# First attention of a four-stage kernel: reciprocals repeated by transfers through DRAM and multiplied by GpSimd, keys stored in three transfers

## What is computed

```
x = x + tanh(g_xattn[0]) * L0_xattn(layernorm(x), ctx, Wq, bq, ..., Wo, bo)
x = x + tanh(g_ffn[0])   * L0_ffn(layernorm(x), ...)
x = x + tanh(g_xattn[1]) * L1_xattn(layernorm(x), ctx, ctx, gamma)
x = x + tanh(g_ffn[1])   * L1_ffn(layernorm(x), ...)
```

```
q, k, v = Wq @ x + bq, Wk @ c + bk, Wv @ c + bv      # each (16 heads, 8, 256)
p   = softmax(q^T k / sqrt(8))                       # (16, 256, 256)
out = Wo @ (v p^T) + bo
```

## Time and profile before

| what | us |
|---|---|
| three runs | 737.46, 737.70, 739.45 (median 737.7) |
| span of the profiled execution | 735.7 |
| TensorE busy in it | 652.3 (89%) |
| VectorE busy | 520.7 (71%) |
| ScalarE busy | 371.1 (50%) |
| GpSimd busy | 343.9 (47%) |
| first attention | about 0 to 262 |

### The profile page before, as it was taken

How to read it: one execution, slowest core, us unless ns; L and a number is a source line. 1 busy time by engine, 2 the same in 40 slices (tenths; PEclk the granted TensorE clock), 3 DMA queues, 4 the chain that set the end, 5 groups by cost and what they waited for, 6 DMA issues and landing times.

```text
span 735.7 us, 13724 instructions
## 1 busy us (share of the span) xinstructions
PE 652.3 (89%) x4738; PEld 343.7 (47%) x4738; DVE 520.7 (71%) x1245; ACT 371.1 (50%) x616; POOL 343.9 (47%) x402
## 2 busy tenths in 40 slices
PE   3889999999999989989853789899988899999996
PEld 1233333333333345778530344444443367777763
DVE  3888989888889479936346889899864864333336
ACT  2047778788777644345421556566642203444420
POOL 3745646657431110177376887642010036777630
PEclk9999999999999999999985889999999999999998
DMA  6945545565632293054563677785218312222237
GB/s 151 208 109 138 144 119 140 155 172 148 173 91 82 58 308 80 1 158 142 187 181 99 184 208 220 193 213 166 71 39 268 84 40 68 88 88 81 71 116 255
DMA packets 110151, 101.12 MB, mean 137 GB/s; under 512 B 26344, under 2 KB 95629, under 8 KB 109611
## 3 DMA queue, kind: packets, MB, share of 16 engines
q1 hardware_dynamic: 100259, 80.52, 39.0%
q0 software_dynamic: 8352, 18.74, 9.2%
q10 hardware_dynamic: 1472, 0.99, 0.6%
HBM read 58.49 MB, written 24.40 MB: 113 GB/s over the span
## 4 chain that ended last, share of the span: by engine, by line
PE 58%; DVE 17%; issue 7%; POOL 7%; DMA 5%; SPq 3%; ACT 2%; POOLq 0%; ACTq 0%; DVEq 0%
PE O L478 10%; PE S L433 10%; PE ST L1567 6%; DVE mx L597 5%; POOL spare L305 4%; PE ST L441 3%; PE ST L1481 3%; PE M L1584 2%; PE S L1584 2%; PE M L527 2%; PE M L520 2%; SPq L170 2%; DMA QS<-mxT 1%; DMA PX<-xn,TI 1%; PE M L1512 1%
## 5 line engine op out<-in xcount | busy, mean ns | idle before, releaser
L597 DVE TENSOR_REDUCE mx<-S 128x2 f32<-128x512 f32 x384 | 251.2, 684 | 37.9 <-PE S L433 36.4
L353 ACT ACTIVATE PX<-ST 128x1024 f32<-128x1024 f32 x192 | 196.2, 1024 | 95.9 <-PE ST L441 91.6
L433 PE MATMUL S<-QS 62*128 62x256 bf16 (+1 forms) x768 | 151.8, 293 | 37.7 <-DVE mx L597 29.9
L441 PE MATMUL ST<-QS 64*128 64x256 bf16 (+1 forms) x768 | 141.1, 278 | 2.6 <-DMA QS<-mxT 2.6
L478 PE MATMUL O<-PX,VA 128*32 128x256 f32 x1536 | 123.9, 395 | 0.1
L433 PEld LDWEIGHTS S<-QS 62*128 62x128 bf16 (+1 forms) x768 | 48.1, 97 | 156.8 <-DVE mx L597 104.7
L305 POOL DMA_INDIRECT spare<-ye,GI x64 | 67.9, 1060 | 25.0 <-issue 12.7
L1685 POOL DMA_INDIRECT PX<-xn,TI x39 | 39.8, 1020 | 54.4 <-DVE K1n L1874 38.9
L441 PEld LDWEIGHTS ST<-QS 64*128 64x128 bf16 (+1 forms) x768 | 54.0, 97 | 17.5 <-issue 9.0
L810 POOL DMA_INDIRECT PX<-xn,TI x32 | 34.1, 1064 | 53.5 <-DVE spare L1196 44.1
L1567 PE MATMUL ST<-EGU,Cb 128*128 x156 | 52.7, 460 | 0.3 <-ACT Cb L1640 0.3
(11 more groups left out here) (299 smaller groups left out, 1111.4 us busy)
## 6 DMA issues: line engine op xcount, KB each, us to landing
QS<-QKs SPq DMA_DIRECT2D x93, 128.0 KB
QS<-keys SPq DMA_DIRECT2D x16, 512.0 KB, 4.7
keys<-spare SPq DMA_DIRECT2D x96, 64.0 KB, 2.1
QS<-QKs SPq DMA_DIRECT2D x93, 64.0 KB
EGU<-in_ew SPq DMA_DIRECT2D x16, 256.0 KB, 4.5
xn<-spare SPq DMA_DIRECT2D x8, 512.0 KB, 10.3
ye<-QKc SPq DMA_DIRECT2D x32, 128.0 KB, 2.1
VA<-in_val SPq DMA_DIRECT2D x16, 256.0 KB, 2.9
```

The costliest lines, as they stand in the source:

```text
L353: e.activation(M["PX"][pair % 4][:, :], M["ST"][pair % 2][:, :], ACT.Exp, scale=A.scale).then_inc(A.exp, 1)
L433: got = e.matmul(M["S"][n % 2][:, 256 * a:256 * a + 256], QS[:, 0, 128 * a:128 * a + 128], QS[:, 1, :], start=True, stop=True)
L441: got = e.matmul(M["ST"][(NP * t + k // 2) % 2][:, 512 * u + 256 * a:512 * u + 256 * a + 256], QS[:, 1, 128 * a:128 * a + 128], QS[:, 0, : ...
L597: e.tensor_reduce(M["mx"][b % 2][:, :, A.row_of_max(head)], M["S"][n % 2][:, :].rearrange("p (a s) -> p a s", a=2), AX.X, ALU.max, negate= ...
```

## The change

For the batches 0 to 13 of the first attention (`by_rows`) the reciprocals go another way. Batches 14 and 15, and the second attention, keep the old one.

- VectorE takes the reciprocals of batch t-1 behind the maximum of k=6 of step t, not those of batch t-2 behind k=0.
- SP stores them to DRAM (`den_d`, 4 rows of 4 KB) at the end of its list of the same step, ahead of the keys.
- In the next step, between the third and the fourth `spread`, SP repeats the 4 rows 8 times each from DRAM to DRAM (`row_d`, 32 rows of 4 KB), where it stored `rT` before. Behind `dn` and `on` it waits for this to have landed and loads `row_d` into `RB`, 128x256.
- GpSimd multiplies `on` by `RB` at the end of its step. The matmul of line 520 and VectorE's multiplication of line 634 are gone.
- `output` stays at k=15 of the same step. `rT` is now the first 16 rows of `RB`.
- The keys are stored by three transfers in place of six. Each repeats one part over 3, 2 or 1 of the rows k. The array in DRAM has k ahead of the rows i, and the loads and the two stores of constants follow it.
- One semaphore (`gates`) is merged into another (`filled`).

```diff
+    def by_rows(self, b):
+        return self.first and 0 <= b < NB - 2
...
 def keys_stored(e, w, A, M, b):
     w.wait_ge(A.keys, 4 * (b + 1))
-    rows = M["keys_d"][b].rearrange("(i k) (g t) -> i g k t", k=8, g=8)
-    for k in range(6):
-        e.dma_start(rows[:, :, k, :], M["KW"][b % 2][:, TERMS[k][1], :]).then_inc(A.kept[b % 2], 16)
+    rows = M["keys_d"][b].rearrange("k i (g t) -> (i g) k t", g=8)
+    for j, lo, hi in ((0, 0, 3), (1, 3, 5), (2, 5, 6)):
+        part = M["KW"][b % 2][:, j, :].unsqueeze(1).to_broadcast([P, hi - lo, T // 2])
+        e.dma_start(rows[:, lo:hi, :], part).then_inc(A.kept[b % 2], 16)
...
 def attention_sp(...):
         def reciprocals():
             w.wait_ge(A.rr, b5 + 1)
-            w.wait_ge(A.rb, b5 - 1)
+            if A.first:
+                w.wait_ge(A.on, b5 - 1)
+            else:
+                w.wait_ge(A.rb, b5 - 1)
             e.dma_start(M["rT"][b5 % 2][0:H, :], M["rdn"][:, 0:2 * H]).then_inc(A.rT, 16)
+        def repeated():
+            w.wait_ge(A.rT, 16 * (b5 + 1))
+            w.wait_ge(A.rows, 32 * (b5 - 1))
+            e.dma_start(M["row_d"][b5 % 2].rearrange("(j i) x -> j i x", j=4),
+                        M["den_d"][b5 % 2].unsqueeze(1).to_broadcast([4, A.R, NQ * T])).then_inc(A.rows, 16)
...
                 spread(e, A, M, b1, k)
-                if k == 2 and within(b5) and A.first:
-                    reciprocals()
+                if k == 2 and A.by_rows(b5):
+                    repeated()
...
+        elif A.by_rows(b5):
+            repeated()
         elif within(b5) and not A.late(b5):
             reciprocals()
...
             e.dma_start(on[b4 % len(on)][:, :], M["OS"][0:P:NQ, 0:NQ, :]).then_inc(A.num, 16)
+        if A.by_rows(b5):
+            w.wait_ge(A.rows, 32 * b5 + 16)
+            w.wait_ge(A.on, b5 - 1)
+            e.dma_start(M["RB"][b5 % 2][:, :], M["row_d"][b5 % 2].rearrange("r (g t) -> (r g) t", g=NQ)).then_inc(A.rows, 16)
...
+        if A.by_rows(b4):
+            w.wait_ge(A.rr, b4 + 1)
+            e.dma_start(M["den_d"][b4 % 2], M["rdn"][:, 0:2 * H]).then_inc(A.rT, 16)
         if A.first and within(t + 1):
             keys_stored(e, w, A, M, t + 1)
...
 def attention_pool(...):
         if A.first and within(t + 2):
             keys(t + 2)
+        b5 = t - 2
+        if A.by_rows(b5):
+            on = M["on" + A.name][b5 % 2]
+            w.wait_ge(A.rows, 32 * (b5 + 1))
+            w.wait_ge(A.num, 16 * (b5 + 1))
+            e.tensor_tensor(on[:, :], on[:, :], M["RB"][b5 % 2][:, :], ALU.mult).then_inc(A.on, 1)
...
 def attention_pe(...):
-                if k == 12 and within(b5):
+                if k == 12 and within(b5) and not A.by_rows(b5):
                     denominators(b5)
...
 def attention_dve(...):
-                if k == 0 and within(b5):
+                if k == 0 and within(b5) and not A.by_rows(b5):
                     reciprocals(b5)
+                if k == 6 and A.by_rows(t - 1):
+                    reciprocals(t - 1)
...
-                if k == 13 and within(b5):
+                if k == 13 and within(b5) and not A.by_rows(b5):
                     normalized(b5)
```

More of the change, by code:

```diff
@@ L96, in __init__ @@
             self.kp, self.yb = one("kp"), one("yb")
+            self.rows = one("rows")
             self.vt, self.va = one("vt"), one("va")
@@ L265, in keys @@
         w.wait_ge(A.ldc[b % U], 16 * (b // U + 1))
-        w.wait_ge(A.kept[b % 2], 96 * (b // 2))
+        w.wait_ge(A.kept[b % 2], 48 * (b // 2))
         w.wait_ge(A.keys, 4 * b)
@@ L518, in denominators @@
         w.wait_ge(A.rT, 16 * (A.n0 + b + 1))
+        if A.first:
+            w.wait_ge(A.on, b)
         bank()
@@ L632, in normalized @@
         w.wait_ge(A.num, 16 * (A.n0 + b + 1))
-        w.wait_ge(A.rb, b + 1)
+        w.wait_ge(A.rb, b + 1 - (NB - 2 if A.first else 0))
         e.tensor_tensor(on[:, :], M1[:, 256:512], on[:, :], ALU.mult).then_inc(A.on, 1)
@@ L732, in __init__ @@
         self.again = [one(f"again{u}") for u in range(E0 - PLACES)]
-        self.again0 = [96 * NB // 2, 96 * NB // 2, 32, 0, 0]
+        self.again0 = [48 * NB // 2, 48 * NB // 2, 32, 0, 0]
         self.at = {}
@@ L751, in ffn0_sp @@
     for k in (6, 7):
-        e.dma_start(M["keys_d"].rearrange("b (i k) x -> k (b i) x", k=8)[k],
-                    d["hole"][:, 3072:4096].to_broadcast([NB * P // 8, 1024])).then_inc(B.kept[2], 16)
+        e.dma_start(M["keys_d"][:, k, :, :],
+                    d["hole"][:, 3072:4096].unsqueeze(1).to_broadcast([NB, P // 8, 1024])).then_inc(B.kept[2], 16)
     w.wait_ge(G.dve, G.at["wd"])
@@ L760, in stack_ready @@
         for k in range(2):
-            w.wait_ge(B.kept[k], 96 * NB // 2)
+            w.wait_ge(B.kept[k], 48 * NB // 2)
         w.wait_ge(B.kept[2], 32)
@@ L2075, in allocate @@
                           ("st6", [P, 6], F32), ("mv", [P, 2], F32), ("ve", [P, 1], F32), ("rs", [P, 1], F32),
-                          ("mx", [P, 2, 16], F32), ("mxT", [16, T], BF16), ("rT", [16, T], F32), ("on", [P, T], F32)):
+                          ("mx", [P, 2, 16], F32), ("mxT", [16, T], BF16), ("RB", [P, T], F32), ("on", [P, T], F32)):
         M[nm] = [sb(f"{nm}{n}", shape, dt) for n in range(2)]
+    M["rT"] = [m[0:16, :] for m in M["RB"]]
     Cbs = sb("Cb", [P, U, T])
@@ L2160, in allocate @@
     M["ye_d"] = nc.dram_tensor("ye", [E0 * CAP + P, T], F32, kind="Internal").ap()
-    M["keys_d"] = nc.dram_tensor("keys", [NB, P, 4 * T], F32, kind="Internal").ap()
+    M["keys_d"] = nc.dram_tensor("keys", [NB, 8, P // 8, 4 * T], F32, kind="Internal").ap()
+    for nm, rows in (("den", 4), ("row", 32)):
+        two = nc.dram_tensor(nm, [2, rows, 4 * T], F32, kind="Internal").ap()
+        M[nm + "_d"] = [two[n] for n in range(2)]
     M["ew_d"] = d["ew"]
@@ L2212, in build @@
         M["n_e"] = 16 * (EARLY + 3)
-        hole, filled, gates, gamma = (sem(nm) for nm in ("hole", "filled", "gates", "gamma"))
+        hole, filled, gamma = (sem(nm) for nm in ("hole", "filled", "gamma"))
         M["hole"], M["gamma"] = hole, gamma
@@ L2299, in act_program @@
             w.wait_ge(M["w_g"], 16)
-            e.activation(M["tg"][:, :], M["graw"][:, 0:4], ACT.Tanh).then_inc(gates, 1)
+            w.wait_ge(filled, 1)
+            e.activation(M["tg"][:, :], M["graw"][:, 0:4], ACT.Tanh).then_inc(filled, 1)
             attention_act(e, w, L0, M, ffn0_act_meanwhile(e, w, X, L0, M))
@@ L2336, in gated @@
                 if t == -3 and k == 1:
-                    w.wait_ge(gates, 1)
+                    w.wait_ge(filled, 2)
                     e.tensor_tensor(M["tg"][:, 2:3], M["tg"][:, 2:3], M["graw"][:, 4:5], ALU.mult).then_inc(gamma, 1)
```

2 lines of the change are left out of this document (1 added, 1 removed).

## The result

The changed kernel takes 758.07 us in the median of four runs (755.32 to 758.79), beside 738.4 for four of the kernel before: a ratio of 1.0257 with a 95% interval of 1.0226 to 1.0289, or 19.7 us slower. Forecast were 749.9 us and a range up to 756. The direction and the main mechanism were right, the size was not.

What follows compares the result with a forecast made beforehand. TensorE and VectorE take turns setting the pace through two banks S. 13 steps, each 1.14 less 0.11 us longer, give 13.4; less 1.2 at the start, +12.2 us: 749.9 us, range 735 to 756.

Steps and rivals of the forecast that it cites:

- Parts 1 and 2: First attention, line 520's matmul and VectorE's multiplication gone: together 0.05 to 0.11 us a step gained, 0.11 taken.
- Part 3: Reciprocals at k=6 wait for the transfer of `dn`: maximum of k=7 1.14 us late in each of 13 steps.
- Part 4: SP's queue: a shorter list ends TensorE's waits for the context at the stage's start, -1.2 us.
- Part 5: The rows' way through DRAM to GpSimd's multiplication: costs nothing, with a cover of 2 us before `output`.
- Part 6: Ends of the first attention (steps 14, 15): zero; second attention with reordered keys: zero, some tenths either way.

Runs made afterwards that it cites:

- e8_no_division: The kernel before without line 520 and VectorE's multiplication for batches 0 to 13, nothing in their place; ratio 1.0015 to the kernel before.
- e1_k7: The changed kernel with the reciprocals behind the maximum of k=7, not k=6; ratio 1.0115 to the kernel before.
- e3_keys_only: The kernel before with the keys' part of the change alone (three transfers, new order in DRAM); ratio 1.0071.
- e14_context_first: The kernel before with SP issuing the next context load ahead of the six key transfers; 734.06 beside 738.46 us, ratio 0.9948.
- e5_roots_first: The changed kernel with GpSimd's square roots for the routing ahead of its multiplication by RB; ratio 1.0275 to the kernel before.
- e4: The changed kernel with the keys' part undone (six transfers, old order); ratio 1.0272 to the kernel before.
- e2: The changed kernel with the reciprocals behind the maximum of k=9, not k=6; ratio 1.0125 to the kernel before.
- e15: The changed kernel with reciprocals behind k=7, roots first, context first and the old keys (six transfers); ratio 1.0096 to the kernel before.
- e10_order_only: The kernel before with the new order of the keys in DRAM alone, still six transfers; ratio 1.0025.
- e12_padded: The kernel before with three key transfers in the new order and planes of 16 rows padded to 17; ratio 1.0014.
- e6: The changed kernel with reciprocals behind k=7 and GpSimd's square roots ahead of its multiplication; ratio 1.0034 to the kernel before.

## Why the prediction was right or wrong

*Parts 1 and 2, little from the removed matmul and multiplication: right.* I took 0.05 to 0.11 us a step; 0.05 was measured in e8_no_division and in e1_k7.

*Part 3, the stall: right in mechanism and, in sum, in size.* The maximum of k=0 in step 14 comes 11.8 us late, beside +12.2 forecast. Its terms were off in ways that cancelled. The landing was 2.05 to 2.3 us (I took 2.3), so steps 2 to 11 are 14.11 to 14.34 us long and not 14.32. The estimate of 2.04 us from the Trainium skill (DMA: Bandwidth & Descriptors, "Anatomy of one DMA — SWDGE (gpsimd) path"), for a transfer issued by GpSimd, is at the short end of what was measured here for SP. Step 12 alone is 15.9 us long, 3.3 more than before and not about 1. There the spreads were late, `dn` was issued right behind them, and landed after 3.1 us, and a fall of the clock followed (last section). The other twelve steps lost 8.9 us where the forecast's terms give 11.2, so that the sum came out near is luck.

*Part 4, SP: too small.* I took 1.2 us from the waits for the context; e3_keys_only and e14_context_first win 1.7 in the first five full steps, and some 2.2 up to the logits.

*Part 5, the rows' way: right for the steps it was worked out for.* GpSimd waited 0.2 us for `RB` between 100 and 200 us. It did not hold for steps 12 to 15, with waits of 3.8 to 6.7 us.

*Part 6, "I count zero" for the ends: this is the step that failed.* From k=0 of step 14 to the last logits the changed kernel loses 4.8 us. I had looked at what VectorE's reciprocal and line 520 do there, not at GpSimd's queue. Part 5's cover, 9.9 us of GpSimd's own work ahead of the multiplication, ends with the last batches, and behind the multiplication stand the roots, which VectorE and TensorE wait for. The rows of the kernel before showed these roots at 233.9, 235.9 and 241.5 us. e5_roots_first takes 5.9 us off this stretch, 2.6 of them idle time of TensorE and an estimated 3.3 two falls of the granted clock, of which only the first is seen to follow a wait for the roots. With the roots first the stretch is 1.1 us shorter than before: the gain from line 520 that I had put at 0.7 is there. That the clock would fall behind a wait stood nowhere in the sum; its three falls in the changed kernel's first attention, where the kernel before has none, are an estimated 5 of the 17.8 us. Its four runs have 0.962 to 0.965 as granted clock, beside 0.970 in the profile before.

*Part 6, "the second attention reads the same bytes from another order: zero": also wrong,* by some 3 us of TensorE's waits in the profiles. The net effect on the run is 1 to 5 us by the four ratios on the keys, two of them clear of 1; of the changed kernel's own 17.8 us, the stages behind the logits have 1.1 in all.

Against the span: 11.8 for the steps, 4.8 for the end, 1.1 in the stages behind, is 17.7 of 17.8 us. The range ended 2 us short, since a wait was priced on the engine that makes it, and neither for its neighbours in another queue nor for the clock behind it.

## What to carry to other kernels

Where two engines hand each other two buffers, work taken from one gives what the slot lets through, here 0.05 of 0.72 us, so walk one period slot by slot before moving work. A result that comes by a transfer needs a place in the queue that is later than its landing: one slot later took 0.9 us a step back. A wait put into an in-order queue is hidden by the work around it only as long as there is such work, so check the last steps of the pipeline, where the work thins out and other things stand behind it. And before two single executions are compared by landmarks, look at the granted clock of both: here it moved a landmark by 1.7 us at a time with no edit near it.

## What the runs showed of the hardware

A wait of TensorE can cost more than itself. In step 12 of the changed kernel the scores of k=9 came after 1.82 us of idle time (timeline), and the granted clock (windows: length, busy us of PE, PEld, DVE, ACT, POOL, clock) fell to 0.50, the level of 1.2 GHz, for 3.4 us:

```profile
218.83 0.28 PE L467 MATMUL S<-QS 62*128 62x256 bf16 x1 [1.82 <-DVE mx L633]
```

```profile
218.00:220.00 2.00, 1.17 (x12) 0.75 (x12) 1.96 (x4) 0.71 (x1) 0.72 (x1) 0.99 0.77 204
220.00:223.40 3.40, 3.40 (x32) 0.97 (x28) 1.96 (x4) 1.80 (x3) 0.00 (x0) 0.50 0.39 122
223.40:226.00 2.60, 2.09 (x29) 0.58 (x25) 2.39 (x4) 1.61 (x3) 0.00 (x0) 1.00 0.03 9
```

With the landing of 3.1 us this is what step 12 lost beyond the other steps. Between 60 us and the last logits the fifteen profiles have seven single waits of TensorE of 1.8 us or more. Around six of them the clock fell, from 0.4 us before the wait's end to 1.8 us after it (1.82, 1.87, 1.90, 2.04, 2.18 and 2.49 us: the changed kernel twice, e4, e5, e1, e2); one of 1.84 us had no fall (e15), nor had nine of 1.0 to 1.7 us. So a long wait and a fall go together here, but not each time, and the falls near the end in e10_order_only, e12_padded, e1_k7 and, the second one, in the changed kernel came behind waits of 0.4 and 0.6 us which other kernels have without a fall. What decides is not shown.

The start of the pipeline shows the clock too. The step between the bias additions of steps -1 and 0 lasts 13.2 to 13.6 us in nine of the fifteen profiles and 15.0 to 15.3 in six, whatever the edit (e5, e6, e8, e10, e14, e15). The record of the granted clock begins at its rise to 1.00, at 45.1 to 47.4 us in the nine and at 51.1 to 52.1 in the six, and eight matmuls of the values take 1.08 us ahead of it and 0.64 behind it. The same eight in e6_k7_roots and in the kernel before:

```profile
48.49 1.08 PE L512 MATMUL O<-PX,VA 128*32 128x256 f32 x8
```

```profile
48.19 0.64 PE L478 MATMUL O<-PX,VA 128*32 128x256 f32 x8
```

Why it rises later in some executions is not shown. It makes single executions differ by 1.8 us in the mean.

One more thing. A load of 512 KB in rows of 4 KB took 4.7 to 4.8 us (medians) when neighbouring partitions read neighbouring rows, and 5.6 to 6.6 when they read rows 64 or 68 KB apart.
